# Last stage of a mixer and mixture-of-experts kernel: the sum of a token's two expert rows on VectorE in place of GpSimd

## What is computed

```python
x = _layernorm(x + mixer(x, W_u, b_u, W_g, b_g, A, Bm, Cm, D))
scores = xt @ gate_w
ew, ei = top_k(scores, 2); ew = softmax(ew)                 # wE[e, t]: weight of expert e for token t, or 0
h = gelu(xt @ w1[e] + b1[e]); o = h @ w2[e] + b2[e]
y = _layernorm(xt + o, ln_g[e], ln_b[e])                     # per expert
x = _layernorm(x + sum_e(wE[e] * y[e]))                      # the last stage of the kernel makes this line
```

## Time and profile before

| what | value |
|---|---|
| median of 3 runs | 295.02 us (294.75 to 295.34) |
| the profiled execution's own time | 295.8 us |
| span of its profile | 294.0 us |
| VectorE busy | 182.0 us of the span (62%), 902 instructions |
| GpSimd busy | 149.6 us of the span (51%), 185 instructions |
| the sums on GpSimd (L1451) | 8 instructions, 10.1 us busy, 1274 ns in the mean |
| weighing of the second rows on VectorE (L1322) | 32 instructions, 10.5 us busy |
| statistics of the sums (L1334) | 32 instructions, 7.1 us busy |
| the last stage, from its first VectorE instruction to its last | 254.17 to 290.27 us |

### The profile page before, as it was taken

One profiled execution on the slowest core, in us unless ns is written; L12 is line 12 of the kernel. 1 busy time (PEld: TensorE's weight loads), 2 busy tenths in 40 slices (PEclk: granted clock), 3 DMA queues, 4 the chain that ended last, 5 costly groups with the idle time before them and its releaser, 6 DMA issues.

```text
span 294.0 us, 5551 instructions
## 1 busy us (share of the span) xinstructions
PE 201.8 (69%) x1223; PEld 152.4 (52%) x1226; DVE 182.0 (62%) x902; ACT 139.1 (47%) x404; POOL 149.6 (51%) x185
## 2 busy tenths in 40 slices
PE   4989998897896533088799999999999970000000
PEld 2567765666554422033588888888888850000000
DVE  1354528879028997925056666766666681399994
ACT  2423335656203303340396777767768610052765
POOL 7000000777775777773037767767767775042330
PEclk9999999996699775559999999999999995555555
DMA  5970000111111111421423343343333110950113
GB/s 174 299 226 12 0 1 2 46 56 56 47 52 44 47 45 56 118 63 47 104 66 94 93 105 92 90 106 89 92 98 86 48 57 12 372 204 1 71 71 143
DMA packets 22372, 25.61 MB, mean 87 GB/s; under 512 B 4388, under 2 KB 16569, under 8 KB 22348
## 3 DMA queue, kind: packets, MB, share of 16 engines
q1 hardware_dynamic: 17958, 16.84, 19.2%
q0 software_dynamic: 4352, 8.50, 8.8%
q10 hardware_dynamic: 38, 0.01, 0.0%
HBM read 14.15 MB, written 11.71 MB: 88 GB/s over the span
## 4 chain that ended last, share of the span: by engine, by line
PE 47%; DVE 24%; POOL 8%; issue 8%; DMA 5%; ACT 5%; SPq 1%; ACTq 0%; POOLq 0%; DVEq 0%
PE bank L720 11%; PE bank L730 10%; POOL y_rows L1437 5%; POOL buckets L1429 4%; DVE by_token L1322 3%; PE bank L447 3%; PE bank L732 3%; PE bank L466 3%; PE bank L448 3%; DVE st L1334 2%; PE bank L707 2%; ACT pay L799 2%; PE bank L539 2%; PE bank L516 2%; DMA by_token<-y_rows 2%
## 5 line engine op out<-in xcount | busy, mean ns | idle before, releaser
L1429 POOL DMA_INDIRECT buckets<-pay,dest x64 | 63.2, 987 | 65.9 <-ACT pay L799 49.1
L1437 POOL DMA_INDIRECT y_rows<-powers_then_yb,row_ids x72 | 70.9, 985 | 41.4 <-DVE powers_then_yb L1287 23.4
L730 PE MATMUL bank<-w_sb,hidden 128*128 x288 | 47.8, 288 | 0.0
L903 ACT ACTIVATE hidden<-bank,bcol 128x128 f32<-128x128 f32 x144 | 41.0, 374 | 7.7 <-PE bank L720 7.6
L720 PE MATMUL bank<-xbT,x_tok 128*128 128x128 f32 x288 | 41.1, 287 | 0.0
L730 PEld LDWEIGHTS bank<-w_sb,hidden 128*128 128x128 f32 x288 | 37.7, 191 | 2.5
L720 PEld LDWEIGHTS bank<-xbT,x_tok 128*128 128x128 f32 x288 | 34.7, 191 | 2.2
L893 ACT ACTIVATE x_tok<-w_sb 128x256 f32 x72 | 26.3, 431 | 0.8 <-issue 0.8
L1287 DVE SCALAR_TENSOR_TENSOR powers_then_yb<-z1T,powers_then_yb,gbc 128x128 f32<-128x128 f32 x72 | 22.3, 350 | 5.7 <-DVE powers_then_yb L1283 0.7
L885 ACT ACTIVATE xbT<-bank 128x512 f32<-128x512 f32 x18 | 10.8, 597 | 29.8 <-PE bank L707 28.7
L942 ACT ACTIVATE by_token<-by_token,scale 128x128 f32<-128x128 f32 (+1 forms) x32 | 9.8, 388 | 29.9 <-DVE scale L1312 29.9
(11 more groups left out here) (169 smaller groups left out, 383.5 us busy)
## 6 DMA issues: line engine op xcount, KB each, us to landing
gates_then_xb<-buckets SPq DMA_DIRECT2D x72, 64.5 KB
by_token<-y_rows SPq DMA_DIRECT2D x8, 520.0 KB, 7.0
x_tok<-in_L_attn_x_dram SPq DMA_DIRECT2D x8, 256.0 KB, 4.8
out_dram<-x1b SPq DMA_DIRECT2D x8, 256.0 KB, 2.5
y_rows<-powers_then_yb,row_ids POOLq DMA_INDIRECT x72, 2.3
w_sb<-in_L_ffn_w_dram SPq DMA_DIRECT2D x1, 1024.0 KB
buckets<-pay,dest POOLq DMA_INDIRECT x64, 2.3
buckets<-pad SPq DMA_DIRECT2D x9, 64.5 KB, 2.6
```

Source lines behind the costliest of these rows:

```text
L730: mm(ps_o[h][:, i * P:(i + 1) * P], hidden[q % 2][:, s, c, :], w2_sb[:, bass.ds(e * (FC * P) + c * P, P)], start=(c == 0), stop=False)
L903: ins = f(hidden[q % 2][:, s, c, :], ps_hid[(q % 2) * 2 + s // 2][:, at:at + P], ACT.Gelu, bias=bcol[:, bass.ds(e[s] * FC + BIAS_ROW + c, 1)])
L1429: pool.indirect_dma_start(buckets, bass.IndirectOffsetOnAxis(ap=dest[:, k, t:t + 1], axis=0), pay[k][:, t, :], None).then_inc(scattered, 16)
L1437: pool.indirect_dma_start(y_rows, bass.IndirectOffsetOnAxis(ap=row_ids[q][:, s:s + 1], axis=0), yb[q][:, s, :], None, bounds_check=TOKENS ...
```

## The change

The loop on GpSimd goes. `weigh_second(r)` gets two more steps behind its 8 weighted rows, one for each group of the round: VectorE waits for both semaphores of the group, adds the first rows to the second ones for the four tiles in one instruction and raises `sums_ready`. Each of the two sums is a step of the generator, so what is drawn beside the weighing goes on between them.

```diff
--- before.py
+++ after.py
@@ -1324,6 +1324,13 @@
                     if j % TPG == TPG - 1:
                         ins.then_inc(t1_ready, 1)
                     yield
+                for g in range(r * (OT // TPG), (r + 1) * (OT // TPG)):
+                    first_rows, second_rows = (yin[:, g * TPG * TOP:(g + 1) * TPG * TOP, 0:P]
+                                               .rearrange("p (j k) d -> p j k d", k=TOP)[:, :, k, :] for k in range(TOP))
+                    dve.wait_ge(t0_ready, g + 1)
+                    dve.wait_ge(t1_ready, g + 1)
+                    tt(second_rows, second_rows, first_rows, ALU.add).then_inc(sums_ready, 1)
+                    yield
 
             def second_statistics(r):
                 if later(r, 1):
@@ -1443,14 +1450,6 @@
                 scatter_batch(b)
 
 
-            with pool.Fori(0, GROUPS) as g:
-                pool.wait_ge(t0_ready, g + 1)
-                pool.wait_ge(t1_ready, g + 1)
-                first_rows, second_rows = (yin[:, bass.ds(g * TPG * TOP, TPG * TOP), 0:P]
-                                           .rearrange("p (j k) d -> p j k d", k=TOP)[:, :, k, :] for k in range(TOP))
-                gp.tensor_tensor(second_rows, second_rows, first_rows, ALU.add).then_inc(sums_ready, 1)
-
-
 # ---- launch: one core; inputs and outputs as the reference has them ----
 _INS = ['L0_attn_x', 'L0_attn_W_u', 'L0_attn_b_u', 'L0_attn_W_g', 'L0_attn_b_g', 'L0_attn_A', 'L0_attn_Bm',
         'L0_attn_Cm', 'L0_attn_D', 'L0_ffn_gate_w', 'L0_ffn_w1', 'L0_ffn_b1', 'L0_ffn_w2', 'L0_ffn_b2',
```

## The result

The kernel became slower: 297.25 us in the median of 20 runs against 295.16 for 20 runs of the kernel before, a ratio of 1.0065 with a 95% interval of 1.0044 to 1.0086. The forecast was 296.5, and 297.25 lies in its range.

The account below looks back on a forecast made before the run. VectorE was taken to bound the last stage. Eight sums there add 4.57 us and 3.07 us of stalls go, together +1.5 us on a median of 295.02: 296.5 us, range 295.7 to 297.5.

Parts of the forecast that it names:

- VectorE bounds the stage: Last stage: it lasts as long as VectorE's instructions, busy 33.31 of 34.98 us; nobody waits for GpSimd's sums.
- What goes: 3.07 us: Last stage: stalls of VectorE's two-input instructions beside GpSimd's sums end: 1.69 us first round, 0.83 second, 0.55 last two.
- What comes: 8 x 0.60: Last stage: eight sums on VectorE at 0.60 us start to start; in the first round two add 0.97 us.
- Round by round: Last stage: first round -0.72 us, second +0.37, third and fourth together +1.85; in all +1.5 us.
- No wait for ScalarE: Sums behind the weighings: in the third round the second sum starts 0.25 us after ScalarE's last row, so no wait.
- The rivals that would have made it faster: Two rivals for the sums: VectorE pays 0.337 us each, 294.4 us (4%); or sums were on the path, 289.6 us (2%).
- a wait for ScalarE: Rival at VectorE's sums: ScalarE's rows come late, about 0.3 us lost in each of three rounds, 297.4 us (7%).

Follow-up runs that it names:

- the first four experiments: Against the kernel before: no sums, 292.54 us; GpSimd adding unused tensors, 297.31; GpSimd only writing, 291.44; against the changed kernel: VectorE summing the first round only, 295.07.

## Why the prediction was right

*VectorE bounds the stage.* Shown. Every kernel of the table that keeps VectorE's order changed by what VectorE's instructions changed by, in both directions, and taking away 10 us of GpSimd's work gave 3.07.

*What goes: 3.07 us.* Shown alone by the run without sums. The reading of it, that instructions with two inputs stand still while GpSimd reads and that the statistics pass, is borne out by the runs with the addition elsewhere and with the fill.

*What comes: 8 x 0.60.* The sum takes 686 ns and stands 0.60 us before the next instruction. One row behind the price was misread: the two instructions over 256 elements that the prediction calls additions (L1249) are multiplications, with one input repeated. It changed nothing, since additions of 128 and 512 elements stand 0.202 and 0.60 apart and a line through these gives 0.335 for 256, where the prediction had 0.337. The stretch from L1008 to L1005 in the first round is 260.57 - 259.20 = 1.37 us, where 1.38 was worked out.

*Round by round.* From the first weighing of one round to that of the next, in the profile after: 4.90 us (256.51 to 261.41), 8.02 (to 269.43) and 8.24 (to 277.67). Before, these weighings started at 256.89, 262.51, 270.16 and 277.48, so the rounds took 5.62, 7.65 and 7.32:

```profile
256.89 0.35 DVE L1322 SCALAR_TENSOR_TENSOR by_token<-by_token,scale,x1b 128x128 f32<-128x128 f32 x1
...
270.16 0.35 DVE L1322 SCALAR_TENSOR_TENSOR by_token<-by_token,scale,x1b 128x128 f32<-128x128 f32 x1
...
277.48 0.35 DVE L1322 SCALAR_TENSOR_TENSOR by_token<-by_token,scale,x1b 128x128 f32<-128x128 f32 x1
```

The differences are -0.72, +0.37 and +0.92, and from the last of these to the last norm 12.60 against 11.67, +0.93. Forecast: -0.72, +0.37 and two times 0.925.

*No wait for ScalarE.* In the third round ScalarE's rows end at 269.64 + 2.45 = 272.09 and the second sum starts at 271.76 + 0.60 = 272.36, 0.27 us behind; 0.25 was forecast.

The rivals that would have made it faster had the wrong price (0.337 against the 0.60 measured) or the wrong path (nobody waits for a sum in either profile).

*What it did not foresee* is 0.6 us of the 2.1 between the two medians. The stage accounts for 1.5 us, 0.5% of the time, which lies in the interval of the ratio. The rest would have to lie ahead of the stage, where the change edits nothing. The start of the stage moves by 3.2 us among four profiles of one kernel, so a difference of 0.6 between two medians of 20 runs can be scatter. The record shows misses of up to 0.9 us, both ways, where a median's change is set beside that of its stage: 0.2 us over it without sums, 0.6 over it with the additions elsewhere, 0.9 under it with the fills, 0.9 over it with the first round on VectorE, 0.1 under it with TensorE. The kernels without sums and with fills have the same stage, 31.91 us, and medians 1.1 us apart. The unedited kernel had medians of 295.44 (24 runs) and 295.47 (11 runs) beside the experiments, 0.3 above the 295.16 of the result. Whether a part of the 0.6 belongs to the changed program was not settled: the timed runs carry no trace.

*What was luck.* That 297.25 lies in the range. The upper end, 297.5, was set by a wait for ScalarE, which did not come; the forecast with the 0.1 that the range gave to the spread of the runs ends at 296.6. The change of the stage was not luck: its four parts came out as they were worked out.

## What to carry to other kernels

When two engines disturb each other, moving work from one to the other is worth the stalls that it ends less the time that it takes on the engine which bounds the stage. Read the stalls as the longest instruction of a line less its median, and price the work by its distance from start to start: here 3.07 against 4.57, though GpSimd needed 1274 ns in the mean for a sum and VectorE 686. Work that no one waits for can go to an engine that does not halt the bound one, as with TensorE here (where the order was changed too), or be placed where the bound engine waits anyway, as in the first round.

## What was not expected

- A GpSimd addition does not always halt VectorE's two-input instructions. In the third and fourth rounds the weighings beside it were not slower, and it took longer itself (up to 1613 ns, 1091 at least); in the second it got in ahead of the last of them and cost 0.83. The same program does the same each time, and what decides it stays open.
- The weighing, which reads a scale for each partition, stands 0.262 us before its successor; a plain addition of the same 128 elements 0.202. That the scale makes the difference was not tried by itself.
- All scatter in the profiled executions lies ahead of the last stage: the time less the start of the stage is 41.60 to 41.63 us in four profiles, while the start moves from 252.82 to 256.04. The time goes with TensorE's granted clock, whose mean over the execution is listed for each run: of the 24 runs of the unedited kernel beside the first four experiments, the nine at 0.853 to 0.858 took 293.89 to 294.96 us, the fifteen at 0.838 to 0.844 took 295.25 to 297.24. Why the clock differs was not tried.
